# Moving the lags of a three-engine edge loop: VectorE sums the block before between a scan and a maximum, TensorE turns values earlier

## What is computed

```python
q = (x @ Wq.T + bq).reshape(N, H, C)      # k and v likewise
logits = (q[dst] * k[src]).sum(-1) * (1.0 / np.sqrt(C))
m = segment_max(logits, dst)
e = exp(logits - m[dst])
denom = segment_sum(e, dst)
out = segment_sum(v[src] * (e / (denom[dst] + 1e-16))[..., None], dst)
return out + x @ Ws.T + bs
```

## Time and profile before

| | us |
|---|---|
| median of three runs | 3877.36 |
| lowest, highest run | 3876.87, 3889.24 |
| the profiled execution's own time | 3880.24 |
| its span, first to last instruction | 3878.5 |
| first gather of layer 0 to the end of its last gather | 211.2 to 1417.9 |
| the same for layer 1 | 1616.1 to 2825.9 |

### The profile page before, as it was taken

How to read it: one execution, slowest core, us unless ns; L and a number is a source line. 1 busy time by engine, 2 the same in 40 slices (tenths; PEclk the granted TensorE clock), 3 DMA queues, 4 the chain that set the end, 5 groups by cost and what they waited for, 6 DMA issues and landing times. The chain is left out here.

```text
span 3878.5 us, 46469 instructions
## 1 busy us (share of the span) xinstructions
PE 2641.4 (68%) x13243; PEld 2233.3 (58%) x13243; DVE 2388.1 (62%) x3615; ACT 1128.4 (29%) x2130; POOL 1955.0 (50%) x1958
## 2 busy tenths in 40 slices
PE   2436656666666664356656666666659999999999
PEld 1324545555545553245545555445549889889998
DVE  3237667777667763266767777667755556556555
ACT  6201111111111111011111111111126666666665
POOL 6466766776767747566666776766720000000000
PEclk9756665666656655566665666666659999999999
DMA  9233434443444432234434444444420000000000
GB/s 382 90 89 113 119 112 115 115 119 113 117 114 115 120 84 53 74 108 119 122 115 120 119 126 119 123 118 120 118 54 13 23 11 13 22 10 13 19 10 10
DMA packets 364383, 356.26 MB, mean 92 GB/s; under 512 B 58758, under 2 KB 297500, under 8 KB 364272
## 3 DMA queue, kind: packets, MB, share of 16 engines
q1 hardware_dynamic: 191552, 167.96, 14.2%
q0 software_dynamic: 62896, 125.63, 12.2%
q10 hardware_dynamic: 109824, 61.36, 5.1%
HBM read 246.48 MB, written 108.30 MB: 91 GB/s over the span
## 5 line engine op out<-in xcount | busy, mean ns | idle before, releaser
L540 POOL DMA_INDIRECT kv<-kv_table,ix x1664 | 1688.7, 1015 | 748.8 <-issue 478.3
L600 DVE TENSOR_TENSOR_SCAN held_q<-mask,held_q,qT 128x512 f32<-128x512 bf16 x208 | 263.7, 1268 | 735.0 <-remote 690.4
L572 PE MATMUL outT<-identity,run_v 128*128 128x128 f32 x832 | 329.5, 396 | 544.8 <-ACT rows L657 490.0
L646 ACT ACTIVATE ex<-gap 128x1024 f32<-128x1024 f32 x208 | 219.9, 1057 | 1294.0 <-issue 804.5
L550 PE MATMUL kT<-identity,kv 128*128 128x128 f32 x832 | 344.6, 419 | 337.9 <-DMA kv<-kv_table,ix 299.1
L572 PEld LDWEIGHTS outT<-identity,run_v 128*128 128x128 f32 x832 | 228.2, 274 | 590.9 <-ACT rows L657 493.1
L557 PE MATMUL logit<-kq,head_sum 128*128 128x512 f32 x416 | 390.8, 1042 | 92.3 <-DVE gap L622 54.6
L1320 DVE TENSOR_TENSOR hid_lo_x<-full_x,hid_hi_x 128x448 fp32r<-128x448 f32 x448 | 276.1, 623 | 258.4 <-ACT hid_hi_x L1206 252.9
L1206 ACT ACTIVATE full_x<-psH_x,offset_x,scale_x 128x448 f32<-128x448 f32 x448 | 332.4, 742 | 296.0 <-PE psH_x L1061 295.9
L574 PE MATMUL restT<-pick,top 128*128 128x8 f32 x1664 | 402.6, 315 | 1.8 <-issue 1.8
L573 PEld LDWEIGHTS restT<-pick,run_d 128*128 128x128 f32 x1664 | 401.9, 293 | 0.0
(11 more groups left out here) (209 smaller groups left out, 5333.8 us busy)
## 6 DMA issues: line engine op xcount, KB each, us to landing
running_sums<-rows ACTq DMA_DIRECT2D x208, 288.0 KB
qz<-q_at_starts SPq DMA_DIRECT2D x208, 256.0 KB
mask<-masks SPq DMA_DIRECT2D x416, 128.0 KB
q_at_starts<-zeros SPq DMA_DIRECT2D x16, 1664.0 KB
kv<-kv_table,ix POOLq DMA_INDIRECT x1664
x_sb<-in_x SPq DMA_DIRECT2D x1, 6272.0 KB
kv_table<-proj SPq DMA_DIRECT2D x14, 448.0 KB
x_x<-in_x POOLq DMA_DIRECT2D x7, 896.0 KB, 5.8
```

The costliest lines, as they stand in the source:

```text
L540: pool.indirect_dma_start(kv[:, u, j, 2 * HC * s:2 * HC * (s + 1)], None, kv_t, bass.IndirectOffsetOnAxis(ix[:, b, n:n + 1], 0)).then_inc( ...
L572: pe.transpose(outT[:, of], run_v[:, u, of], identity[:, :])
L600: dve.tensor_tensor_scan(held_q[:, h, :], mask[:, u, 0, :], qT[h][:, :], held_q[:, 1 - h, STEP - 1:STEP], ALU.mult, ALU.add).then_inc(q_he ...
```

## The change

`each_block` now takes pairs of a stage and its lag, so a stage may stand anywhere in the pass. TensorE's pass becomes turn_kq of b, turn_v of b-1, logits of b, turn_results of b-2. VectorE's pass becomes hold_q of b, sums of b-1, maximum of b. ScalarE keeps weights of b and store of b-2. No instruction is added or taken away in the loop, and no buffer and no wait condition is altered. GpSimd's and SyncE's code is the same.

```diff
                     def blocks(i):
                         for u in range(U):
-                            for lag, stage in enumerate(stages):
+                            for stage, lag in stages:
                                 b = U * i + u - lag
                                 if not isinstance(i, int) or b >= U * past:
                                     stage(b, (u - lag) % U, i if u >= lag else i - 1)
                     each_step(eng, body)
-                    for late in range(1, len(stages)):
-                        for lag in range(late, len(stages)):
+                    for late in range(1, max(lag for _, lag in stages) + 1):
+                        for stage, lag in stages:
                             b = U * (past + STEPS) + late - 1 - lag
-                            stages[lag](b, b % U, b // U)
+                            if lag >= late:
+                                stage(b, b % U, b // U)
...
-                    each_block(pe, [turn_kq, logits, turn_v, turn_results])
+                    each_block(pe, [(turn_kq, 0), (turn_v, 1), (logits, 0), (turn_results, 2)])
...
-                    each_block(dve, [hold_q, maximum, sums], after=part_low)
+                    each_block(dve, [(hold_q, 0), (sums, 1), (maximum, 0)], after=part_low)
...
-                    each_block(act, [weights, lambda b, u, i: None, store], before=part_high)
+                    each_block(act, [(weights, 0), (store, 2)], before=part_high)
```

## The result

The changed kernel takes 3919.22 us (median of 4 runs, 3909.74 to 3920.07) against 3877.11 us for the kernel before (median of 4). The ratio is 1.0106, with a 95% interval of 1.0091 to 1.0121: slower by 42 us. The profiled execution of after took 3918.96 us; its span is 38.7 us longer than that of before.

The account below looks back on a forecast made before the run. No engine was full; GpSimd's gathers, plus pauses while TensorE's signals are held back, bound the edge loops. The profiled 3880.2 + 33 (single blocks) + 5 (layer ends) = 3918 us, 3915 as median; own range 3892 to 3950, 8-in-10 range 3755 to 3955.

Parts of the forecast that it names:

- One block a cycle: GpSimd's edge-loop gathers: v's signal misses its wait, so it pauses after every block, not every two; 11.86 us a block against 11.64.
- The term of +33 us: Edge loops: pausing after single blocks costs 0.22 us on some 200 blocks, 44 us, less a quarter.
- the quarter that was taken off the 44 us: Edge loops: reduction of the cost of pausing after every block, from 44 to 33 us.
- The start pause: Start of each layer's edge loop: GpSimd's 5.15 us pause shrinks to 1.8 to 2.4 us, -3 us a layer.
- The ends: Behind each layer's last gather: three passes remain instead of two, 38.3 us to the last store; +7.6 and +3.0 us.
- The logits signal: TensorE to VectorE, at +4.0 us of a pass: passes within the first 8 us, so costs nothing.
- TensorE's chain of 9.6 us a block: Loop of hold_q, logits, results, k and q: 9.6 us, covered by GpSimd's 10.05 us a block.
- VectorE's pass of before: VectorE's edge-loop work when fed: 8.19 us a pass, unchanged by the change.
- the signs: Edge-loop trace: GpSimd pauses 1.8 us after every block, over 150 remote waits; VectorE waits 2.5 to 3.5 us nearly every pass.
- GpSimd no longer pauses: Rival: earlier v ends the edge loop's pauses wholly (3630 us) or half (3755 us); chance 0.20 for wholly or in part.
- Pairs stay, nothing else changes: Rival: GpSimd still pauses after every two blocks; 3865 to 3889 us, chance 0.22; with a small gain 0.12.
- The working model of late signals: While GpSimd issues indirect DMAs in a row, TensorE's signals pass for some 8 us, then hardly until the row ends.

Follow-up runs that it names:

- e11: Changed kernel with the sums' factor ex1 written to PSUM, rerun on a chip with late signals: 3921.2 us, 1.0116 times before.
- e9: Changed kernel's stage order with the lags of the kernel before, on a chip with late signals: 3891.75 us, 1.0039 times before.
- e3: Changed kernel without the gathers of k and v; SyncE loads a fixed block by one plain DMA instead: 3335.61 us.
- e4: Kernel before without the gathers of k and v; SyncE loads a fixed block by one plain DMA instead: 3102.86 us.
- e7: Changed kernel with the sums' factor ex1 written to PSUM, on a chip without late signals: 3528.34 us, 0.981 times before.
- e2: Kernel before with run_d scanned ahead of the product wv, so the two sums no longer stand back to back: 3721.5 us, 1.0326 times before.
- e10: Changed kernel with both the factor ex1 and the difference of the maxima in PSUM, on a chip with late signals: 3920.84 us, 1.0112 times before.
- e12: Changed kernel with ex1 in PSUM and v turned a block earlier, on a chip without late signals: 3536.08 us, 0.9818 times before.
- e8: Kernel before with GpSimd waiting after each block's eight gathers until they have landed: 4219.79 us.

## Why the prediction was right, and where it was not

The forecast was 3915 us, in a range of its own from 3892 to 3950. The time is 3919, and the sign is right. That the number fits is luck for the most part: the largest term, +33 us for single blocks, did not come about, and another of +25 us that was put at nothing stood in its place.

- **One block a cycle** is the step that failed. The prediction had v end at +10.7 us and GpSimd at its wait at +10.05, and let signals pass for the first 8 us only. v ended at +10.25, and its signal passed at once (in 72 rows the trace has it within 0.05 us). GpSimd came to the wait at +10.84, because a gather beside the sums had been held. The pairs stayed. The pattern itself is real: e11 shows it on 192 rows, 11.81 us a block with pauses of mostly 1.5 to 2.2, where 11.86 was read from the earlier trace rows. It came when the sums no longer held a gather; that this was for a lost race between v and GpSimd is borne out in 45 rows and not in the other 146.
- **The term of +33 us** was thus put down to the wrong thing. In its place stand +41.5 us of held gathers, less 16.4 us of pauses: +25. No run shows the quarter that was taken off the 44 us: in layer 0's edge phase the granted clock was 0.55, lower than the 0.61 of before, and the pairs stayed, 94 of them against 90. The prediction saw that something lengthens the gathers (1.015 against 0.95) and did not ask how the new place of the sums would move them against the gathers. Its own sum had room for them: 1045 of 1207 us a layer leave 324 us in two layers, it says that the rest is pauses, and those are 249.6. The other 74 are the held gathers, 101 us, less 28 of issue time that falls into the pauses. The order rows could have pointed to a new place of the sums against the gathers, since they stand right behind q's scan and the product there. The size they do not give; e9 finds 22 of the 41.5 us from the order and 19 from the shorter lags.
- **The start pause** did not shrink to 1.8 to 2.4 us. It is 5.59 us, behind five blocks, where it was 5.15 behind four. A missing -6 us.
- **The ends** were right in kind and a little short. VectorE makes three passes after the last gather of layer 0, as said. From that gather to the last store it is 40.8 us (38.3 forecast, 30.7 before), in layer 1 41.4 (35.2 before): +10.1 and +6.2, where +7.6 and +3.0 were forecast. Of these, +8.7 and +3.9 reach the next gather and the end of the span. On the other kind of chip these last two were 4.3 and 2.4 us shorter than before.
- **The logits signal** passed in the first 8 us, as said. TensorE's chain of 9.6 us a block was measured at 9.4 (e3), VectorE's pass of before at 8.2 (e4), and the gathers cover both, as said.
- **Of the signs** named, the waits of VectorE at nearly every pass were seen, but at 1.7 and 5.4 us by turns. Those of GpSimd, over 150 remote waits and 1.8 us after every block, were not (99).
- **The rivals.** "GpSimd no longer pauses" is untrue on the chip of the prediction. On the chips without late signals it is true of both kernels, and even there the change costs 1%. "Pairs stay, nothing else changes" was right on the pairs, and short of the held gathers and the tails.
- **The working model of late signals** is only half shown. It belongs to some chips, or to a state of theirs, and not to the kernel alone: the same kernel had 105 such pauses on one and none on another. Where it holds, its window is not fixed at 8 us. In after, signals of v passed at +10.3 us. In 89 rows the logits ended between +11.9 and +13.8 and were in use at most 1.8 us later, without a wait, while most of the signals of +16 and later came with the bundle at +23.3. In e11 the signals of v that ended at +9.5 to +10.5 came at +11.5. What makes them late no run here has shown. That it goes with indirect DMAs the traces do show: in before each of the 318 waits marked remote ends during one or within 5.4 us of the last one's end, and in the 363 us behind the last of them engines wait 109 times for TensorE, never remote.

## What to carry to other kernels

When GpSimd issues indirect DMAs in a row and bounds a loop, count the VectorE instructions with both inputs in SBUF, and look at what their timeline does to the gathers that start in them. Give one of the inputs a place in PSUM (e7: 1.9% less than before), and where that can't be, stand them back to back (e2: 3.3% more when they were pulled apart). But e7's kernel was 1.2% slower than before on the other kind of chip (e11), where the pauses grew by what the gathers lost. So where engines wait for one another, compare a change on more than one chip before its gain or loss is put down to a cause.

## What the runs showed of the hardware

- A gather of 128 rows takes 0.951 to 0.954 us on GpSimd and 0.304 us of issue. One that starts while VectorE runs an instruction with two SBUF inputs ends 0.76 us after a scan's end and 0.825 us after a subtraction's or an addition's (0.816 where that writes to PSUM, e10), with a spread of 2 to 3 ns in each of the twelve traces with gathers. Those that start in its first 0.05 to 0.09 us or its last 0.15 to 0.2 us take 0.95 as ever. Instructions that read one of their inputs from PSUM held none: q's scan and the maximum's none of the 196 to 222 that start in each, in any of the twelve, and run_d and run_v none of 170 to 200 in each of e7, e10, e11 and e12.
- The scans are not slowed by this (run_d 1.28 us in after, where 141 gathers were held beside it, 1.27 in e7 with one input in PSUM and none held): only GpSimd pays.
- Two kinds of chip, or two states of chips, at 3875 and 3600 us for one kernel, with VectorE's scans (1.27 us) and an undisturbed gather (0.95) of one length on both; the difference that the traces show is in when TensorE's signals arrive. At 814.75 to 814.94 us in before all four of its signals of the edge loop are recorded within 0.19 us, 6.7 to 11.7 us after the last instruction that each stands for.
- Eight gathers of 64 KB each have landed 3.6 us after the last one's end (e8: 737.3 us in 206 waits).
